# A fused network in float32 on one core: the max rows go out on SP's queue, and turns, projections and banks of the attention stage move

## The reference

```
x = x + zX*lap_x(x) + zY*lap_y(x) + zR*x*(1-x)         # diffusion step
x = x + sum over 8 experts + 1 shared of gate * (silu(x@Wg) * (x@Wu)) @ Wd
x = x + LoRA(x, language) + lang_embed
q = (side + b_self) @ Wq;  k = [x + b_prev, side + b_self] @ Wk;  v = [x, side] @ Wv
score_prev = q.k_prev * SCALE, masked by length        # 128 x 128 per batch and head
score_self = q.k_self * SCALE                          # one per query
w = softmax([score_prev, score_self]);  attn = w_prev @ v_prev + w_self * v_self
x = x + attn @ Wo + bo
```

## Time and profile before

| | us |
|---|---|
| median of 3 runs | 488.98 (486.17 to 490.18) |
| the profiled execution's own time | 490.55 |
| its span | 488.7 |
| PE busy | 441.0 (90%) |
| DVE busy | 341.5 (70%) |
| ACT busy | 273.2 (56%) |
| POOL busy | 210.9 (43%) |

### The profile page before, as it was taken

One profiled execution on the slowest core, in us unless ns is written; L12 is line 12 of the kernel. 1 busy time (PEld: TensorE's weight loads), 2 busy tenths in 40 slices (PEclk: granted clock), 3 DMA queues, 4 the chain that ended last, 5 costly groups with the idle time before them and its releaser, 6 DMA issues.

```text
span 488.7 us, 7752 instructions
## 1 busy us (share of the span) xinstructions
PE 441.0 (90%) x2278; PEld 330.3 (68%) x2278; DVE 341.5 (70%) x594; ACT 273.2 (56%) x544; POOL 210.9 (43%) x261
## 2 busy tenths in 40 slices
PE   5789699779999998999999999999999778888894
PEld 2668578567678787867878686787787354545552
DVE  5787567597777779677768967776796666565552
ACT  2647556546465555545565554556556546565573
POOL 4667666883223434222244323228557333243340
PEclk9889979989999999999999999999999898797798
DMA  5423322300002020000201000022025256555320
GB/s 155 128 72 108 124 66 83 110 23 22 2 0 87 1 67 0 21 0 0 83 3 53 11 0 1 0 65 67 0 67 145 56 158 171 134 128 139 78 58 23
DMA packets 28147, 30.68 MB, mean 63 GB/s; under 512 B 4084, under 2 KB 22616, under 8 KB 28120
## 3 DMA queue, kind: packets, MB, share of 16 engines
q1 hardware_dynamic: 26664, 29.99, 21.8%
q0 software_dynamic: 1024, 0.26, 0.3%
q10 hardware_dynamic: 432, 0.10, 0.1%
HBM read 22.73 MB, written 7.35 MB: 62 GB/s over the span
## 4 chain that ended last, share of the span: by engine, by line
PE 63%; DVE 13%; DMA 8%; ACT 6%; issue 5%; POOL 4%; DVEq 0%; ACTq 0%; SPq 0%; POOLq 0%
PE acc_ps L516 6%; PE g_ps L516 5%; PE acc_ps L518 5%; PE g_ps L518 5%; PE acc_ps L517 5%; PE g_ps L517 5%; DVE act_lo L1086 5%; PE u_ps L516 5%; PE u_ps L518 4%; PE u_ps L517 4%; DMA w_raw<-in_L_cond_Wu 4%; DVE act_p L1082 3%; DMA q_blocks<-max_rows 3%; PE pv_ps L694 2%; PE s_ps L585 2%
## 5 line engine op out<-in xcount | busy, mean ns | idle before, releaser
L815 ACT ACTIVATE act_p<-g_ps 128x512 f32<-128x512 f32 x144 | 86.0, 597 | 135.2 <-PE g_ps L518 120.5
L1082 DVE TENSOR_TENSOR act_p<-act_p,u_ps 128x512 f32<-128x512 f32 x144 | 98.6, 685 | 71.5 <-PE u_ps L518 44.5
L1086 DVE TENSOR_TENSOR act_lo<-act_p,act_hi 128x512 fp32r<-128x512 f32 x144 | 121.1, 841 | 0.2 <-ACT act_hi L820 0.2
L1296 POOL TENSOR_TENSOR xg_lo<-xg,xg_hi 128x512 fp32r<-128x512 f32 x35 | 50.5, 1442 | 147.1 <-ACT xg_hi L825 147.1
L820 ACT ACTIVATE act_hi<-act_p 128x512 fp32r<-128x512 f32 x144 | 89.8, 624 | 3.8 <-DVE act_p L1082 3.5
L516 PE MATMUL acc_ps<-act_hi,w_split 128*128 128x512 f32 x144 | 62.0, 430 | 16.8 <-DVE act_lo L1086 16.7
L516 PE MATMUL g_ps<-x_hi,w_split 128*128 128x512 f32 (+1 forms) x144 | 57.8, 402 | 1.4 <-DVE x_lo L1112 1.4
L518 PE MATMUL acc_ps<-act_hi,w_split 128*128 128x512 f32 x144 | 57.2, 397 | 0.0
L516 PE MATMUL u_ps<-xg_hi,w_split 128*128 128x512 f32 x144 | 57.0, 396 | 0.1
L518 PE MATMUL g_ps<-x_hi,w_split 128*128 128x512 f32 (+1 forms) x144 | 56.9, 395 | 0.0
L517 PE MATMUL g_ps<-x_lo,w_split 128*128 128x512 f32 (+1 forms) x144 | 56.9, 395 | 0.0
(11 more groups left out here) (161 smaller groups left out, 718.2 us busy)
## 6 DMA issues: line engine op xcount, KB each, us to landing
k_blocks<-k_rows SPq DMA_DIRECT2D x32, 96.0 KB
q_plain<-q_rows SPq DMA_DIRECT2D x8, 384.0 KB
q_blocks<-q_rows SPq DMA_DIRECT2D x32, 96.0 KB
k_plain<-k_rows SPq DMA_DIRECT2D x8, 384.0 KB
w_raw<-in_L_cond_Wg SPq DMA_DIRECT2D x8, 256.0 KB, 2.7
w_raw<-in_L_cond_Wu SPq DMA_DIRECT2D x8, 256.0 KB, 2.9
w_raw<-in_L_cond_Wd SPq DMA_DIRECT2D x8, 256.0 KB, 2.8
q_rows<-rows_hi SPq DMA_DIRECT2D x16, 128.0 KB
```

The lines of the kernel that those rows point to most:

```text
L815: activation(act_p[k % 3][:], g_ps[k % 3][:], ACT.Silu).then_inc(silu_done, 1)
L1082: tt(act_p[k % 3][:], act_p[k % 3][:], u_ps[k % 3][:], ALU.mult).then_inc(prod_done, 1)
L1086: tt(act_lo[k % 3][:], act_p[k % 3][:], act_hi[k % 3][:].bitcast(F32), ALU.subtract).then_inc(act_lo_done, 1)
L1296: tt(xg_lo[e % 3][:], xg[:].rearrange("p b s -> p (b s)"), xg_hi[e % 3][:].bitcast(F32), ALU.subtract)\
```

## The change

SP takes over `place_max` for all batches, and its list is now a loop over batches. The maxima of b+1 are turned and copied in body b, behind its first score product, instead of those of b+2 at the end. `turn_attn` and `copy_attn` move ahead, `project` moves ahead of the last `scores_t`, so that other products stand between. The last tile's five steps use `out_ps`. The own weight is kept as a ninth column beside the own values (`own_w`), so that `normalise` adds numerator and denominator in one instruction. POOL weighs the own values before it splits the next maxima.

```
@@ sync
-            for p in range(NP + 3):
-                if p == 2:
-                    later_stores(NT - 1)
-                if p == NP - 4:
-                    sp.wait_ge(rows_stored, ROW_STORES * 2 * NT)
+            step(0)
+            for b in range(B):
+                sp.wait_ge(max_copied, b + 1)
+                place_max(b)              # the two DMAs, now sp.dma_start
+                if b % 2 and b > 1:
+                    p = b // 2
+                    if p == NP - 4:
+                        sp.wait_ge(rows_stored, ROW_STORES * 2 * NT)
+                    step(p)
+                if b == LAST_STORES:      # 3
+                    later_stores(NT - 1)
+            for p in range(NP, NP + 3):
                 step(p)
@@ tensor, later_step: ps = later_ps(t), out_ps for the last tile; last_tile_step:
-                    pe.wait_ge(max_copied, b + 2)
@@ tensor, body
+                if s_next:
+                    scores(b + 2, n + 2, 0)
+                if n >= 1 and turn_next:
+                    turn_max(b + 1, n + 1)
+                scores_t(b, n, 0)
+                if s_next:
+                    scores(b + 2, n + 2, 1)
+                scores_t(b, n, 1)
                 last_tile_step(b, 1)
                 if n >= 1:
                     weigh(b - 1, n - 1, 0)
                     weigh(b - 1, n - 1, 1)
+                if n == 2:
+                    pe.wait_ge(aux_drained, LAST_STEP + 4)
+                if n >= 2:
+                    turn_attn(b - 2, n - 2)
...
                     weigh(b - 1, n - 1, 3)
                 if n >= 2:
-                    turn_attn(b - 2, n - 2)
+                    project(b - 2, n - 2)
                 scores_t(b, n, 3)
                 last_tile_step(b, 3)
-                if n >= 2:
-                    project(b - 2, n - 2)
                 if n >= 1:
                     turn_pv(b - 1, n - 1)
-                if isinstance(b, int) and b < 2:
-                    pe.wait_ge(aux_drained, LAST_STEP + (1 if b == 0 else 4))
-                if s_next:
-                    turn_max(b + 2, n + 2)
@@ scalar, body
                 exp_scores(b, n, 0)
+                if n >= 1 and turn_next:
+                    copy_max(b + 1, n + 1)
+                    exp_self(b + 1, n + 1)
                 exp_scores(b, n, 1)
...
                 place_values(b, n)
+                if n >= 2:
+                    copy_attn(b - 2, n - 2)
                 exp_scores(b, n, 2)
...
-                if n >= 2:
-                    copy_attn(b - 2, n - 2)
                 exp_scores(b, n, 3)
-                if s_next:
-                    copy_max(b + 2, n + 2)
-                    exp_self(b + 2, n + 2)
@@ vector, normalise
-                tt(denom[n % 2][:], pv[:, :, DH], self_exp[n % 4][:], ALU.add)
-                tt(numer[n % 2][:], pv[:, :, 0:DH], v_self_w[n % 2][:], ALU.add)
-                nc.vector.reciprocal(rdenom[n % 2][:], denom[n % 2][:])
+                tt(numer[n % 2][:], pv[:, :, 0:DH + 1], own_w[n % 4][:], ALU.add)
+                nc.vector.reciprocal(rdenom[n % 2][:], numer[n % 2][:, :, DH])
@@ gpsimd, body
+                weigh_self(b, n)
                 if s_next:
                     split_max(b + 2, n + 2)
-                weigh_self(b, n, s_next)
-                if s_next:
-                    place_max(b + 2, n + 2)
                     pick_mask(b + 2, n + 2)
```

More of the change, by code:

```diff
@@ L191, in build @@
         self_arg = [sb2(f"self_arg{n}", [128, H]) for n in range(2)]
-        self_exp = [sb2(f"self_exp{n}", [128, H]) for n in range(4)]
-        SMALLS = 2 * (GI * GJ + GI * GJ + GI * GJ + 2 * H + S + H) + 4 * H
+        own_w = [sb2(f"own_w{n}", [128, H, DH + 1]) for n in range(4)]
+        SMALLS = 2 * (GI * GJ + GI * GJ + GI * GJ + 2 * H + S + H) + 4 * H * (DH + 1)
         k_blocks, q_plain, q_blocks, k_plain = [], [], [], []
@@ L210, in build @@
         pv_own = [sb2(f"pv_own{n}", [128, HALVES, S]) for n in range(2)]
-        v_self_w = [sb2(f"v_self_w{n}", [128, H, DH]) for n in range(2)]
-        denom = [sb2(f"denom{n}", [128, H]) for n in range(2)]
         rdenom = [sb2(f"rdenom{n}", [128, H]) for n in range(2)]
-        numer = [sb2(f"numer{n}", [128, H, DH]) for n in range(2)]
+        numer = [sb2(f"numer{n}", [128, H, DH + 1]) for n in range(2)]
         attn = [sb2(f"attn{n}", [128, H, DH]) for n in range(2)]
@@ L351, in placed, with later_ps @@
             return (b - n) * 16 + 32 * (n // 2 + 1)
+        def later_ps(t):
+            return out_ps if isinstance(t, int) and t == NT - 1 else aux_ps
         def wait(eng, semaphore, value):
@@ L478, in store_out, with place_max @@
                              x3[:].rearrange("p t b s -> p (t b) s")[:, p * PAIR:(p + 1) * PAIR]).then_inc(out_stored, 16)
+            def place_max(b):
+                for c in range(2):
+                    sp.dma_start(q_blocks[b // 2 % 2][ROWS + c:ROWS + c + 1, :, :, b % 2 * S:(b % 2 + 1) * S]
+                                 .rearrange("p j i s -> p (j i) s").bitcast(F32),
+                                 max_rows[b % 2][c * H:(c + 1) * H]).then_inc(max_placed[b % 2], 16)
             def step(p):
@@ L558, in later_step @@
                 pe.wait_ge(aux_drained, later_of(t, m))
-                kind = LATER_AUX[m]
+                kind, ps = LATER_AUX[m], later_ps(t)
                 if kind == "lora_a":
                     pe.wait_ge(acc_drained, t + 1)
-                    last = mm(aux_ps[0:64, :], lora_a_t[:], x1[:, t].rearrange("p b s -> p (b s)"), start=True, stop=True)
+                    last = mm(ps[0:64, :], lora_a_t[:], x1[:, t].rearrange("p b s -> p (b s)"), start=True, stop=True)
                 elif kind == "lora_b":
-                    last = mm(aux_ps[:], lora_b_t[:], low_sel.rearrange("p b s -> p (b s)"), start=True, stop=True)
+                    last = mm(ps[:], lora_b_t[:], low_sel.rearrange("p b s -> p (b s)"), start=True, stop=True)
                 elif kind == "key":
                     pe.wait_ge(in_lo_ready, t + 1)
-                    last = three(aux_ps[:], w_qkv_h[:, 1], w_qkv_l[:, 1], in_hi[:], in_lo[:])
+                    last = three(ps[:], w_qkv_h[:, 1], w_qkv_l[:, 1], in_hi[:], in_lo[:])
                 elif kind == "value":
@@ L570, in later_step @@
                         tok = slice(b * S, (b + 1) * S)
-                        last = three(aux_ps[:, tok], in_hi[:, tok], in_lo[:, tok], w_qkv_h[:, 2], w_qkv_l[:, 2])
+                        last = three(ps[:, tok], in_hi[:, tok], in_lo[:, tok], w_qkv_h[:, 2], w_qkv_l[:, 2])
                 else:
                     for b in range(TB):
-                        last = turn(aux_ps[:, b * S:(b + 1) * S], x3_t[:, b], ident)
+                        last = turn(ps[:, b * S:(b + 1) * S], x3_t[:, b], ident)
                 last.then_inc(aux_written, 1)
@@ L717, in last_tile_step, with body @@
                 if isinstance(b, int) and (b, i) in LAST_AUX:
-                    pe.wait_ge(max_copied, b + 2)
                     later_step(LAST_AUX[b, i], NT - 1)
-            def body(b, n, s_next=True):
-                for i in range(2):
-                    if s_next:
-                        scores(b + 2, n + 2, i)
-                    scores_t(b, n, i)
+            def body(b, n, s_next=True, turn_next=True):
+                if s_next:
[6 more added lines that the diff above has]
+                scores_t(b, n, 1)
                 last_tile_step(b, 1)
@@ L757, in _ @@
             for b in range(B - 2, B):
-                body(b, b % TB, s_next=False)
+                body(b, b % TB, s_next=False, turn_next=b + 1 < B)
             for i in range(GI):
@@ L907, in exp_self @@
                 act.wait_ge(self_arg_ready, b + 1)
-                activation(self_exp[n % 4][:], self_arg[n % 2][:], ACT.Exp).then_inc(self_exp_done, 1)
+                activation(own_w[n % 4][:, :, DH], self_arg[n % 2][:], ACT.Exp).then_inc(self_exp_done, 1)
             def exp_scores(b, n, i):
@@ L939, in last_tile_step, with body @@
                     later_step(LAST_AUX[b, i], NT - 1)
-            def body(b, n, s_next=True):
+            def body(b, n, turn_next=True):
                 exp_scores(b, n, 0)
+                if n >= 1 and turn_next:
+                    copy_max(b + 1, n + 1)
+                    exp_self(b + 1, n + 1)
                 exp_scores(b, n, 1)
@@ L966, in _ @@
             for b in range(B - 2, B):
-                body(b, b % TB, s_next=False)
+                body(b, b % TB, turn_next=b + 1 < B)
             take_pv(B - 1, B - 1)
@@ L1345, in _ @@
                         nc.gpsimd.memset(tile[:].bitcast(F32), constant).then_inc(blocks_filled, 1)
[L1348 to L1353, removed]
             def split_max(b, n):
```

36 lines of the change are left out of this document (15 added, 21 removed).

## The result

| | before | after |
|---|---|---|
| median of 4 runs each, taken side by side, us | 489.58 (486.17 to 490.23) | 504.81 (504.08 to 505.88) |
| ratio, with its 95% interval | | 1.0327 (1.0275 to 1.038) |
| span of the profiled execution, us | 488.7 | 502.3 |
| PE / DVE / ACT / POOL busy, us | 441.0 / 341.5 / 273.2 / 210.9 | 439.1 / 337.4 / 271.8 / 192.7 |

Times are medians of all runs; ratios and intervals leave out runs in a slower state, among them two far-off ones, of 826.56 us in the first experiment and 2297.66 us in the fourth.

A forecast was written before the change was run, and what follows sets the result against it. The second stage was taken as bound by small max-row transfers sharing engines with large ones, and by the low clock after stalls. Steps summed to 497.7 against a 488.7 span, +9.0 on 488.98: 498.0 us, own range 492 to 503.

The forecast's parts named there:

- it gets worse still: Rival, chance 0.10: stores and step 2 delay each other, or a step takes 12 us rather than 10.6; 505 us.
- the upper bound for the max rows: Rows on SP's queue land only after everything sent before them plus some tenths; the lower bound was 1.7 us.
- SP's max rows land in 2 to 5 us while blocks are under way: Sign that the prediction is wrong; pairs of 10 to 11.6 us were the other.
- Start: Batch 0's rows go behind step 0: `scores_t(0, 0)` moves 3.3 us later to 382.4, body 2 begins at 398.4.
- 1 us for the bank: Gain in bodies 0 and 1 together from waits that the bank change removes, between 0 and 2.9 us.
- Step 1 and the key stores: Step 1 sent at 400.8, blocks 8.4 us, key stores 8.3 us; `scores_t(4, 0)` at 418.4 against 408.2, +10.2 us.
- near 10: Sign in the profile after: a wait of several us before `scores_t(4, 0)`, near 10, the longest of the stage.
- Pairs: Second stage, each pair bound by a circle through SP's step: 12.0 us with step 2, 13.2 us with steps 3 to 5.
- Pair 12 and the tail: Step 6 loads half, so its pair takes 11.7 us, 7.0 of it at the low clock; from body 14 on 16.0 us.
- The faster one: Rival, chance 0.22: SP's rows slip past blocks and stores, pairs of 11.6 us, body 4's wait under 3 us; 479 us.
- Only the stores let them pass: No-change rival, chance 0.15: rows pass the key stores, `scores_t(4, 0)` starts at 409.8; 489.4 us.
- about 1.4 us: Loss from turning the maxima in the next body rather than at the end of the body before, counted in the sum.

The follow-up runs named there:

- the first experiment: Changed kernel, but POOL sends the max rows on its own queue and SP keeps the changed order of its steps: 489.01 us, ratio 1.0037 to the kernel before.
- the fourth: Kernel before, but SP sends the max rows with the changed kernel's SP list, maxima turned at the end of the body as before: 504.87 us, ratio 1.0318.

## Why the prediction was right, and where its sizes were off

**The time and its luck.** The forecast was 498.0 with a range of its own of 492 to 503. The measured 504.81 lies above that, and at the 505 of the rival "it gets worse still". But that rival's mechanism didn't show: no step took 12 us (the even rows landed 10.3 to 10.9 us after a step's first send), and step 2 was sent at 427.12, when the stores had ended. So the agreement with 505 is chance. And that the forecast was off by no more than 6.8 us is in part luck too: the early terms were too small and the last one too large.

**The parts, one after the other.** The experiments form a path from the kernel before to the changed one; each step is worked out as a quotient of two ratios, so it carries the uncertainty of both, about 1%.

| step | from | to | factor |
|---|---|---|---|
| gap, bank, `normalise`, POOL's order | 1 | 0.9884 | 0.988 |
| maxima turned in the next body | 0.9884 | 1.0166 | 1.029 |
| SP's blocks released by the copy | 1.0166 | 1.0037 | 0.987 |
| rows sent on SP's queue | 1.0037 | 1.0327 | 1.029 |

The order of the steps matters. With SP as the sender the early turn gives 1.0318 and the late one, with the small moves, 1.0327: behind the queue hardly anything of the late turn is seen. And with the early turn the sender's factor is 1.048, not 1.029.

**The mechanism held.** The prediction took the upper bound for the max rows, the landing of all that SP sent before. The wait that moved with the stores shows it, and so do the packets of batch 4's rows, 8 of which came through only as the stores ended, where POOL's passed them. The prediction's own sign of being wrong was badly chosen: "SP's max rows land in 2 to 5 us while blocks are under way" came true by its letter (4.3 to 4.9 us from the send), and yet the theory holds. SP is busy sending a step for some 5.5 us before it sends the rows (440.19 to 445.70 at step 3), so rows that wait for the whole step still land that soon after their own send. "DMA: Bandwidth & Descriptors" of the Trainium skill, section "Queues, rings and completion order", has a row's descriptors consumed in order on each DMA engine; by that rule these rows stand behind the blocks and stores, and the trace agrees. The same page of the Trainium skill, in "Issuing engines are not separate DMA queues", has it that DMAs issued from several engines run on the same DMA engines, so that spreading them saves only issue time. For a small, urgent transfer the measurement decides otherwise: the sender alone moved the time by a factor of 1.048, from 0.9846 to 1.0318 of the kernel before. How much of that lies in SP's list and how much in the queue was not tried apart; for batch 4 the trace has 8.2 us from the copy to the send and 7.0 from there to the landing.

**Start: mis-sized, and the largest miss.** Forecast: `scores_t(0, 0)` at 382.4 and body 2 at 398.4. Measured: 384.75 and 402.89, 4.5 us more. Of these, 1.1 is stage one, whose last product ended later in this execution (379.96 against 378.82). The rows landed 3.8 to 4.8 us after their sends, which is 1.2 more than I gave them. The rest, 2.2, is in the LoRA chain and body 1: after 4.39 us of waiting the granted clock of the stretch was 0.63, and the two LoRA products took 1.97 us. I had let body 0's delay pass on one for one and had subtracted 1 us for the bank; here the stall ahead of the chain also made the chain slower (the same two products took 1.07 us where the first rows went out early). Sending the first rows earlier gave 4.1 to 4.7 us back.

**Step 1 and the key stores: right within 1.4 us.** Forecast 2.4 us from the product to the blocks' send; measured 405.47 - 402.89 = 2.6. Blocks and stores: 16.7 forecast, 17.5 measured (405.47 to 423). Bodies 2 and 3 took 21.4 us against 20.0. The wait "near 10" was 10.62. Two small terms of this sum had no row behind them. One is 0.1 us for SP to wake; SP's send began 0.03 us after the copy (batch 5: 425.91 and 425.94). The other is 0.5 for landing, with 0.4 for the sends; the product came 1.2 us after the stores' end.

**Pairs: three of four near, the first wrong.** Forecast 12.0 and three times 13.2; measured 13.37, 13.22, 14.04 and 13.20. Step 2 has no output store, and yet its pair was as long: the blocks went out 2.9 us after the product, and the rows behind them landed in 4.8 us, at 437.5, 10.4 us after the first block's send where I had 9.4. With the store, steps 3 to 5 took 10.6, 10.9 and 10.3. It adds little, then; I had priced it at 1.4 us.

**Pair 12 and the tail: 3.5 us too long in the forecast.** I took the lower clock for one body after the stall at body 12, 11.7 us; the granted clock of that pair was full, 9.4 us. The tail took 14.8 against 16.0.

**The sum.** 4.5 at the start, 1.4 in bodies 2 and 3, 2.2 in the pairs, less 3.5 behind them, is 4.6: the span's +13.6 against the +9.0 forecast. The medians give +15.2, as the profiled execution was 1.0 us above the median before (490.55) and 0.7 below it after (504.08).

**The rivals.** The faster one, 479 us, rested on rows that don't wait in the queue. The experiment nearest to it, POOL's sends in the changed kernel, gave 489.0, so the rival was priced 10 us too low: even on a queue of their own, rows turned in body b and sent amid blocks land 3 us after their send (up to 6.0) and are late at most bodies. Its own test, body 4's wait under 3 us, failed at 10.62. "Only the stores let them pass" falls by the same wait, and the packets show how near it was: 24 of 32 did pass. The prediction put the later turn at "about 1.4 us", "in the sum". That is the size of the delay of one copy (1.2 us in body 8); it comes back in every body, and where the queue isn't in the way it costs 14 us by ratios. And "what the engines gain in a body is swallowed" fits the changed kernel, but the small moves are worth 1.2% once nothing swallows them.

## What to carry to other kernels

A small transfer that an engine waits for should not share a queue with bulk loads or stores: count what the sender has to send before it, in its list and in its queue, not its own size. When the two are on different queues, try to hold back the bulk instead: here, releasing the blocks behind the odd batch's copy, while they still came in time, gained about 1.5%. And test the parts of a bundled change separately: here two gains of about 1.2% and 1.3% were hidden under two losses of about 2.9%, each known to about 1%.

## What the runs showed of the hardware

- While the key stores run, from 416 to 423 us of the changed kernel, the mean busy share of the DMA engines is 0.28 and the rate is 97 GB/s. Of rows sent meanwhile on the same queue 24 of 32 packets come through at once and 8 only at the end; on another queue all 32 come through, 6 us before the stores end.
- The granted clock of a pair didn't follow the length of the wait before it. Behind waits of 1.90, 2.88, 3.31 and 2.10 us (bodies 6, 8, 10, 12 of the changed kernel) the pairs had 0.87, 0.94, 0.81 and 1.00.
- The same 8 KB rows land in 1.8 to 1.9 us from SP and in 1.7 at best from POOL when nothing else moves, so neither sender's own speed makes the difference.
